# Chunked loads ahead of the last pass, context scaling on GpSimd, PSUM copies on VectorE, and one ring of score banks in a transformer block

## Chip, cores and metric

The kernel runs on one core of one Trainium2 chip, as one launch. The metric is the device time of one execution in microseconds. The profile comes from one profiled execution of the same program on the same kind of core.

## What is computed

One layer of a transformer on an input of 4 batches, 512 positions and 512 features, all float32: attention with 32 query heads in 8 groups of 4 (one key/value head each, head size 16) and a gated feed-forward part of width 1376, both with a layer norm ahead and a residual behind.

```python
q, k, v = split(layernorm(x) @ Wq), split(layernorm(x) @ Wk), split(layernorm(x) @ Wv)
q, k = q * cos + rotate_half(q) * sin, k * cos + rotate_half(k) * sin
att = einsum('bhgqd,bhkd->bhgqk', q, k) / sqrt(16)          # causal mask
x = x + (softmax(att) @ v) @ Wo
xt = layernorm(x)
return x + (silu(xt @ W_gate.T) * (xt @ W_up.T)) @ W_down.T
```

## The kernel before

It has two phases. Phase 1 makes the attention of all four batches, and, in its last pass, the output projection, residual, layer norm and transposition of batch 0. Phase 2 runs the feed-forward part of batch b together with the output projection of batch b + 1. Each float32 operand of the dense products is split in a high part that TensorE reads in one pass (`fp32r`) and the rest, and a product is three matmuls.

**Passes, groups, slots.** `iteration(b, has_next)` is written once for each engine, and the five engines run their own copies. Pass b has 8 groups (one key/value head each, numbered n = 8b + g, so 0 to 31), and a group has 4 slots (`slot = 4g + i`). All order is written by hand: tables name the slot in which a piece of work stands, and an engine works strictly in its own order. In slot i of group n, TensorE (PE) makes the transposed scores of group n for key chunk i (`scores_t`, L1148, into the three-bank ring `ps_t`), the untransposed scores of group n + 2 (`scores`, L1116, into `ps_s`), and in two of the slots the products of the probabilities with V (`weighted_v`, L1161, into `ps_o`). Between them stand pieces of dense work, placed by `gap`: projections of the next batch (L1068, one unit of 12 matmuls per group in groups 0 to 5 or so of a pass), or in pass 3 (batch index B - 1 = 3, groups 24 to 31) the output projection of batch 0 (L1089), from its third group on. Groups 24 and 25 hold no dense pieces.

**The maximum.** VectorE (DVE) reads each bank of `ps_s` for the row maxima of group n + 2 (`row_max`, L872 and L876, 11 banks a group). ACT rounds the 16 maxima of group n + 1 to bf16 (`max_high`), DVE makes the rest (`max_low`, L883, after the first `row_max` of a group), PE transposes both by a matmul with the identity (`transposed_max`, L1132: 32 columns of weights, 128 moving), ACT copies the result (`m_t`, L730), and SP sends it by DMA into rows 96 and 97 of `q_rows` (`stage_max`, L447, slot 1 of a group). Group n + 1 can't begin its `scores_t` until that transfer has landed. ACT takes the exponentials out of `ps_t` (L737), and GpSimd (POOL) masks the diagonal (`mask_probs`, L643 and L645).

**What the change touches.** SP issues all transfers of the loop in one queue, in its written order: `stage_rows` (six DMAs, L434 and L437), `stage_max`, `store_o` (L453), `store_rotated`, and in pass 3 `prepare_batch_0`: at slot 0 the 1 MB of `wo` (L467), two residual tiles (L187) and tile 0 of the attention output with its inverse sums (`load_o`: 8 DMAs of 64 KB, L181 and L182), at slots 4, 8 and 12 the next tiles, at slot 14 the first gate and up weights (L474). DVE scales a tile of that output by the inverse sums (`scale_ctx`, L194, slots 5, 9, 13, 17), ACT makes the high part (L199), DVE the rest (L204). ACT empties `ps_o` (`o_evacuate`, L747) and makes the high part of the transposed x (`xt_high`, L669), DVE its rest (L851).

**Banks.** Banks of `ps_s` are numbered within a group: bank = position % 3, and since a group has 11 positions the first two of a group follow their last users more closely than the rest:

```python
def last_in_bank(k):
    if k >= S_BANKS:
        return k - S_BANKS
    return max(n for n in range(BANKS_OF) if n % S_BANKS == k) - BANKS_OF
```

## Time and profile before

| | |
|---|---|
| median of 3 runs | 793.6 us (790.62 to 796.33) |
| the profiled execution's own time | 795.12 us |
| its span, first to last instruction | 793.4 us |
| granted TensorE clock, mean | 0.978 |
| PE busy | 756.0 us, 95% |
| PE weight loads busy | 510.8 us, 64% |
| DVE busy | 440.7 us, 56% |
| ACT busy | 342.2 us, 43% |
| POOL busy | 211.5 us, 27% |
| phase 1, up to the first matmul of phase 2 | 392.2 us |

The span runs from the first to the last instruction of the profiled execution, and its own time is 1.7 us longer. Busy shares are means over two phases that have different limits, so a stretch must be read by itself. The end of a matmul is modelled: what it really takes, when others follow at once, is the distance from its start to the next start.

### The profile page before, as it was taken

The page shows a single profiled execution, that of the slowest core. Times are in us where ns is not written, and L with a number is a line of the kernel's source. Part 1 is how long each engine was busy: PE and PEld are TensorE (multiplying, and loading weights), DVE is VectorE, ACT ScalarE, POOL GpSimd, SP SyncE. Part 2 cuts the span into 40 slices and gives each one's busy share as a digit, 9 for nine tenths or more (in the row PEclk, how much of TensorE's full clock was granted, in tenths as well). Part 3 has the DMA queues.
Part 4 walks back from the last instruction along what each step waited for, and adds up shares of the span by engine and source line. Part 5 has one row for each costly group of instructions (what it writes and reads, how often), then busy time and mean ns, then how long its engine had stood idle before and what let it go on. Part 6 is the DMA issues. An engine that isn't in the chain of part 4 may idle for free.

```text
span 793.4 us, 12117 instructions
## 1 busy us (share of the span) xinstructions
PE 756.0 (95%) x4209; PEld 510.8 (64%) x4240; DVE 440.7 (56%) x984; ACT 342.2 (43%) x684; POOL 211.5 (27%) x384
## 2 busy tenths in 40 slices
PE   5889999999999997999799999999999999999998
PEld 4634544544444543444488888888888888788886
DVE  6897888688877786898345553233323243241112
ACT  3427767766876776667643322111121111121111
POOL 4236764477446763244300000000000000000000
PEclk9859999999999999799999999999999999999999
DMA  7337676234323435361276200512004120020001
GB/s 264 107 93 241 212 247 209 75 88 121 117 78 100 118 90 189 113 210 42 83 221 205 74 27 4 170 40 80 27 1 162 50 79 26 0 107 0 1 1 53
DMA packets 74613, 81.84 MB, mean 103 GB/s; under 512 B 8720, under 2 KB 58384, under 8 KB 74352
## 3 DMA queue, kind: packets, MB, share of 16 engines
q1 hardware_dynamic: 73264, 79.98, 31.9%
q10 hardware_dynamic: 1296, 1.18, 0.5%
q8 instruction: 30, 0.49, 0.3%
q14 instruction: 23, 0.19, 0.1%
HBM read 57.02 MB, written 33.36 MB: 114 GB/s over the span
## 4 chain that ended last, share of the span: by engine, by line
PE 50%; DVE 0%; issue 0%; DVEq 0%
PE bank L1504 34%; PE ps_y L1556 15%; PE bank L1543 1%; DVE x_in L1486 0%; DVEq L1485 0%
## 5 line engine op out<-in xcount | busy, mean ns | idle before, releaser
L737 ACT ACTIVATE probs<-ps_t 128x512 f32<-128x512 f32 (+1 forms) x352 | 184.2, 562 | 88.5 <-PE ps_t L1148 88.1
L872 DVE CUSTOM_DVE_ANT_0 ps_s<-ps_s,mask_row 128x512 f32<-128x512 f32 (+1 forms) x240 | 145.4, 643 | 43.8 <-PE ps_s L1116 42.7
L1116 PE MATMUL ps_s<-k_rows,q_rows 96*128 96x256 bf16 (+3 forms) x512 | 146.9, 316 | 3.2 <-DVE m_raw L876 1.5
L1461 DVE TENSOR_TENSOR h<-h,bank 128x512 f32<-128x512 f32 (+1 forms) x44 | 30.3, 688 | 214.1 <-PE bank L1504 212.8
L1148 PE MATMUL ps_t<-q_rows,k_rows 98*128 98x512 bf16 (+1 forms) x352 | 129.1, 371 | 8.6 <-DMA q_rows<-m_t 5.8
L1399 ACT ACTIVATE h<-bank 128x512 f32<-128x512 f32 (+1 forms) x44 | 26.3, 597 | 146.3 <-PE bank L1504 146.3
L1161 PE MATMUL ps_o<-probs,v_ones 128*32 128x512 f32 (+3 forms) x1024 | 82.6, 441 | 4.6 <-ACT o_sb L747 0.2
L645 POOL TENSOR_SCALAR_AFFINE_SELECT probs<-probs 128x512 f32<-128x512 f32 x128 | 84.0, 657 | 0.0
L876 DVE TENSOR_REDUCE m_raw<-ps_s 128x2 f32<-128x512 f32 (+3 forms) x112 | 73.3, 678 | 17.4 <-PE ps_s L1121 15.2
L1405 ACT CAST h_hi<-h 128x512 fp32r<-128x512 f32 (+1 forms) x44 | 27.3, 620 | 126.6 <-DVE h L1461 126.6
L226 POOL TENSOR_TENSOR var_eps<-mean_var,eps 128x1 f32<-128x1 f32 x16 | 3.0, 189 | 285.6 <-DVE mean_var L221 285.6
L1116 PEld LDWEIGHTS ps_s<-k_rows,q_rows 96*128 96x128 bf16 x512 | 49.8, 101 | 40.9 <-issue 10.8
L1148 PEld LDWEIGHTS ps_t<-q_rows,k_rows 98*128 98x128 bf16 x352 | 34.6, 99 | 63.6 <-issue 29.3
L643 POOL TENSOR_TENSOR carrier<-half 128x1 f32<-128x1 f32 x128 | 29.0, 227 | 152.3 <-ACT probs L737 151.9
L1556 PE MATMUL ps_y<-wd_hi,h_hi 128*128 128x512 f32 (+1 forms) x176 | 68.8, 391 | 0.0
L1556 PE MATMUL ps_y<-wd_lo,h_hi 128*128 128x512 f32 (+1 forms) x176 | 68.5, 389 | 0.0
L1556 PE MATMUL ps_y<-wd_hi,h_lo 128*128 128x512 f32 (+1 forms) x176 | 68.5, 389 | 0.0
L1161 PEld LDWEIGHTS ps_o<-probs,v_ones 128*32 128x32 f32 x1024 | 27.0, 110 | 43.3 <-issue 31.9
L1504 PE MATMUL bank<-xt_hi,wg_hi 128*128 128x512 f32 (+1 forms) x128 | 50.0, 390 | 0.0
L1504 PE MATMUL bank<-xt_hi,wg_lo 128*128 128x512 f32 (+1 forms) x128 | 49.9, 390 | 0.0
L1504 PE MATMUL bank<-xt_hi,wu_lo 128*128 128x512 f32 (+1 forms) x128 | 49.9, 390 | 0.0
L1504 PE MATMUL bank<-xt_lo,wu_hi 128*128 128x512 f32 (+1 forms) x128 | 49.9, 390 | 0.0
(154 smaller groups left out, 1374.8 us busy)
## 6 DMA issues: line engine op xcount, KB each, us to landing
scratch_o<-o_sb SPq DMA_DIRECT2D x31, 256.0 KB, 2.2
q_rows<-scratch_q_parts SPq DMA_DIRECT2D x32, 192.0 KB
x_in<-in_x SPq DMA_DIRECT2D x16, 256.0 KB, 4.6
q_rows<-scratch_q_parts SPq DMA_DIRECT2D x32, 128.0 KB
x_res<-in_x SPq DMA_DIRECT2D x16, 256.0 KB, 2.7
o_in<-scratch_o SPq DMA_DIRECT2D x64, 64.0 KB
inverse<-scratch_inverse SPq DMA_DIRECT2D x64, 64.0 KB
out<-x_in SPq DMA_DIRECT2D x16, 256.0 KB, 2.0
```

Of the source, the lines that this page charges most:

```text
L643: nc.gpsimd.tensor_tensor(carrier[:, g % 2, c:c + 1], half[:, 0:1], half[:, 0:1], ALU.add)
L645: nc.gpsimd.affine_select(out=diagonal, in_=diagonal, compare_op=ALU.is_ge, fill=0.0, base=0, pattern=[[0, GROUP], [1, P]], channel_multip ...
L737: nc.scalar.activation(probs[:, g % 2, heads * u:heads * (u + 1), CHUNK_AT[c]:CHUNK_AT[c + 1]], ps_t[:, pos % S_BANKS, 0:heads * CHUNK_N[c ...
L872: nc.vector.tensor_tensor_reduce(out=bank, in0=bank, in1=mask_row[:, T - width:T], scale=1.0, scalar=LOWEST, op0=ALU.add, op1=ALU.max, acc ...
L876: nc.vector.tensor_reduce(out=m_raw[:, g % 2, at:at + heads], op=ALU.max, axis=AXIS.X, in_=bank.rearrange("p (j t) -> p j t", j=heads)).th ...
L1116: mm = nc.tensor.matmul(bank[:, place], q_rows[r][0:ROWS, j, P * q:P * (q + 1)], k_rows[r][0:ROWS, 0:width], start=(place == 0), stop=mask ...
L1148: nc.tensor.matmul(ps_t[:, pos % S_BANKS, 0:heads * width], k_rows[r][:, P * c:P * (c + 1)], q_rows[r][:, heads * u:heads * (u + 1), P * c:T],
L1161: mm = nc.tensor.matmul(ps_o[32 * j:32 * j + 2 * DH, P * c:T], v_ones[:, c, g % NKV, :], probs[:, g % 2, j, CHUNK_AT[c]:CHUNK_AT[c + 1]], ...
L1405: nc.scalar.copy(h_parts[0][0:m, r], h[0:m, r]).then_inc(h_hi_ready, 1)
L1461: nc.vector.tensor_tensor(h[0:m, r], h[0:m, r], bank[units["up", f] % BANKS][0:m, :], ALU.mult).then_inc(h_ready, 1)
L1504: mm = nc.tensor.matmul(out, weights(w, c), moving(m, c), start=(c == 0 and n == 0), stop=(c == chunks - 1 and n == 2))
L1556: mm = nc.tensor.matmul(ps_y[:, t], h_parts[w][0:m, r, P * t:P * (t + 1)], wd[p][0:m, f, :], start=(f == 0 and k == 0), stop=(f == FT - 1 ...
```

## The change

- **Loads.** In the pass before the last (`b == B - 2`, batch index 2) SP now issues `wo` in four parts at slots 14, 15, 22 and 23, tiles 0 and 1 of the attention output chunk by chunk (two DMAs a chunk) at slots 2, 3, 6, 7, 10, 11, 18 and 19, and two residual tiles at slots 27 and 31. In pass 3, tiles 2 and 3 come chunk by chunk at slots 9 to 11 and 13 to 15, and the first gate and up weights in four parts at slots 2, 3, 6 and 7.
- **Engines.** `scale_ctx` of phase 1 runs on GpSimd instead of DVE, in the same slots. In pass 3 DVE makes both parts of the transposed x, and copies `ps_o` for groups 29, 30 and 31.
- **Banks.** Banks of `ps_s` form one ring over all groups: bank = (11n + position) % 3.
- **Maximum.** `m_parts` gets six further parts of zeros, so that `transposed_max` has 128 columns of weights; it stands behind the dense piece of its place, not ahead of it; `max_low` stands behind the second `row_max`.
- **Slots.** Layer norm statistics, means and applications, one `rotated` step and the inversion of the sums stand in other slots.

```diff
+LAST_O = {26: 5, 30: 6}
+X_SLOT, MEAN_SLOT = 26, 14
+STATS_AT, APPLY_AT = {6: 0, 7: 1, 10: 2, 11: 3}, {18: 0, 19: 1, 22: 2, 23: 3}
+SUMS_SLOT, INVERSE_SLOT = 7, 18
+WO_LOAD, RESIDUAL_LOAD = (14, 15, 22, 23), (27, 31)
...
-FFN_LOAD, FFN_HI, FFN_LO = 14, 19, 25
+FFN_LOAD, FFN_HI, FFN_LO = (2, 3, 6, 7), 19, 25
...
+def s_place(n, i, u):
+    return BANKS_OF * n + BANK_AT[i] + u
...
-        m_parts = sb("m_parts", [P, 2, 2, GROUP, TT], BF16)
+        m_parts = sb("m_parts", [P, 2, P // (GROUP * TT), GROUP, TT], BF16)
...
+            def prepare_first_tiles(slot):
+                if slot in WO_LOAD:
+                    c = WO_LOAD.index(slot)
+                    if c == 0:
+                        sp.wait_ge(raw_copied, 13 * DMA)
+                    sp.dma_start(to.wo[1][:, c].bitcast(F32), d["wo_raw"][P * c:P * (c + 1)]).then_inc(wo_loaded, DMA)
+                if slot in RESIDUAL_LOAD:
+                    load_residual(sp, d, to, 0, RESIDUAL_LOAD.index(slot))
+                for t, c in O_LOAD_AHEAD.get(slot, ()):
+                    if (t, c) == (0, 0):
+                        sp.wait_ge(inverse_stored, DMA)
+                    load_o_chunk(sp, d, to, 0, t, c)
...
+                    if not has_next and (slot - CTX_SCALE) % TT == 0 and 0 <= slot - CTX_SCALE < TT * TT:
+                        scale_ctx(pool, to, 0, (slot - CTX_SCALE) // TT)
...
+            def last_xt(kc):
+                unit = LAST_UNIT0 + TT + kc
+                dve.wait_ge(dense_ready, unit + 1)
+                nc.vector.tensor_copy(xt_hi[:, kc], dense_bank(unit)).then_inc(xt_hi_ready, 1)
+                xt_low(B, kc, unit)
+
+            def last_output(g):
+                dve.wait_ge(pv_done, NKV * (B - 1) + g + 1)
+                if g < NKV - 1:
+                    dve.wait_ge(o_stored[g % 2], DMA * (NKV // 2 * (B - 1) + g // 2))
+                nc.vector.tensor_copy(o_tile(B - 1, g), ps_o[:]).then_inc(o_evacuated, 1)
...
-                        others.insert(0, lambda: max_low(n + 1))
+                        others[0:0] = [lambda: None, lambda: max_low(n + 1)]
...
-                before = BANKS_OF * n + last_in_bank(BANK_AT[i] + u) + 1
+                before = s_place(n, i, u) - S_BANKS + 1
...
-                nc.tensor.matmul(to[0:2 * GROUP * TT, 0:P], m_parts[:, n % 2].rearrange("p w j q -> p (w j q)"),
+                nc.tensor.matmul(to[:, 0:P], m_parts[:, n % 2].rearrange("p w j q -> p (w j q)"),
```

TensorE's order in group 17, before, from the last scores of slot 0 to the first matmuls of slot 1 (`w_hi` and `w_lo` mark the dense piece, `m_parts` the transposition of the maxima):

```order
L1116 MATMUL ps_s<-k_rows,q_rows 128x512
L1132 MATMUL ps_t<-ident_b,m_parts 32x128
L1068 MATMUL ps_d<-xt_hi,w_hi 128x512
L1068 MATMUL ps_d<-xt_lo,w_hi 128x512
L1068 MATMUL ps_d<-xt_hi,w_lo 128x512
L1148 MATMUL ps_t<-q_rows,k_rows 128x384
```

And the same place in the changed kernel:

```order
L1151 MATMUL ps_s<-k_rows,q_rows 128x512
L1103 MATMUL ps_d<-xt_hi,w_hi 128x512
L1103 MATMUL ps_d<-xt_lo,w_hi 128x512
L1103 MATMUL ps_d<-xt_hi,w_lo 128x512
L1167 MATMUL ps_t<-ident_b,m_parts 128x128
L1183 MATMUL ps_t<-q_rows,k_rows 128x384
```

The transposition has moved behind the dense piece, and writes 128 partitions instead of 32.

The SP queue before, from the end of the row loads in slot 0 of pass 3 (group 24) to the maxima of slot 1 (`q_rows<-m_t`); between the shown pairs on `o_in` and `inverse` stand three more of the same:

```order
L437 DMA q_rows<-scratch_q_parts 16x4x512
L467 DMA wo_lo<-scratch_wo_raw 128x4x512
L187 DMA x_res<-in_x 128x512 x2
L181 DMA o_in<-scratch_o 128x1x128
L182 DMA inverse<-scratch_inverse 128x1x128
```

```order
L181 DMA o_in<-scratch_o 128x1x128
L182 DMA inverse<-scratch_inverse 128x1x128
L447 DMA q_rows<-m_t 2x16x128
L453 DMA scratch_o<-o_sb 128x512
L434 DMA k_rows<-scratch_k_parts 48x1x512
```

The same place in the changed kernel, on to the row loads of slot 4:

```order
L449 DMA q_rows<-scratch_q_parts 16x4x512
L459 DMA q_rows<-m_t 2x16x128
L465 DMA scratch_o<-o_sb 128x512
L496 DMA w_lo<-scratch_wg_raw 128x384
L496 DMA w_lo<-scratch_wu_raw 128x384
L496 DMA w_lo<-scratch_wg_raw 128x384
L496 DMA w_lo<-scratch_wu_raw 128x384
L446 DMA k_rows<-scratch_k_parts 48x1x512
```

The eleven issues between the row loads and the maxima are gone from there, and four parts of the feed-forward weights stand behind the store of the output.

## Rows read from the trace of the kernel before

**Rows 1.** The chain that ended last, by line (page, part 4), and its first long piece.
```profile
PE bank L1504 34%; PE ps_y L1556 15%; PE bank L1543 1%; DVE x_in L1486 0%; DVEq L1485 0%
...
392.21 11.14 PE bank L1504 x48
```

**Rows 2.** Timeline of PE (start us, us, instruction, [idle before <-releaser]): groups 23 to 26 begin.
```profile
296.67 0.39 PE L1148 MATMUL ps_t<-q_rows,k_rows 98*128 98x512 bf16 x1
...
304.79 0.39 PE L1148 MATMUL ps_t<-q_rows,k_rows 98*128 98x512 bf16 x1
...
318.80 0.61 PE L1148 MATMUL ps_t<-q_rows,k_rows 98*128 98x512 bf16 x1 [5.81 <-DMA q_rows<-m_t]
...
330.27 0.39 PE L1148 MATMUL ps_t<-q_rows,k_rows 98*128 98x512 bf16 x1
```

**Rows 3.** Stretches: the two halves of group 25, group 26, group 16.
```profile
core 0: us, PE busy (x) PEld busy (x) DVE busy (x) ACT busy (x) POOL busy (x), PEclk, DMA share, GB/s
...
318.80:326.80 8.00, 8.00 (x34) 2.94 (x35) 6.23 (x18) 4.76 (x11) 0.78 (x2) 0.50 0.39 114
326.80:330.27 3.47, 3.32 (x31) 1.51 (x29) 3.44 (x8) 3.23 (x7) 1.71 (x5) 0.99 0.25 88
330.27:341.15 10.88, 10.73 (x78) 5.27 (x76) 9.90 (x26) 6.84 (x15) 4.48 (x10) 1.00 0.49 144
...
223.21:233.90 10.69, 10.54 (x79) 5.36 (x76) 7.19 (x20) 8.32 (x18) 1.87 (x6) 1.00 0.27 83
```

**Rows 4.** Timeline of the SP queue: last issue of group 23, then group 24.
```profile
300.09 0.67 SPq L447 DMA_DIRECT2D q_rows<-m_t  x1
...
306.06 0.43 SPq L467 DMA_DIRECT2D wo_lo<-scratch_wo_raw  x1
...
314.61 1.15 SPq L447 DMA_DIRECT2D q_rows<-m_t  x1
```

**Rows 5.** DMA issues by line: size of one, median us from issue to landing.
```profile
w_lo<-scratch_wg_raw SPq DMA_DIRECT2D x1, 768.0 KB, 4.7
```

**Rows 6.** Timeline of PE around a transposition of maxima, and later in that group 16.
```profile
225.47 0.38 PE L1116 MATMUL ps_s<-k_rows,q_rows 96*128 96x512 bf16 x1
225.78 0.23 PE L1132 MATMUL ps_t<-ident_b,m_parts 128*32 128x128 bf16 x1
225.94 0.50 PE L1068 MATMUL ps_d<-xt_hi,w_hi 128*128 128x512 f32 x1
226.28 0.39 PE L1068 MATMUL ps_d<-xt_lo,w_hi 128*128 128x512 f32 x1
...
231.50 0.33 PE L1116 MATMUL ps_s<-k_rows,q_rows 96*128 96x128 bf16 x3
231.67 0.38 PE L1148 MATMUL ps_t<-q_rows,k_rows 98*128 98x512 bf16 x1
```

**Rows 7.** Weight loads by line: duration min/median/max, first and last start.
```profile
L1132 PEld LDWEIGHTS ps_t<-ident_b,m_parts x31: 92/93/102, 58.5 to 375.0; 128*32 128x32 bf16 x31
...
L1121 PEld LDWEIGHTS ps_s<-mask_q,ident_b x112: 97/98/152, 40.1 to 371.2; 128*128 128x128 bf16 x112
```

**Rows 8.** GpSimd and VectorE operations by line, columns as in the group above.
```profile
L568 POOL TENSOR_TENSOR rot<-rot,turned x17: 1263/1278/1288, 39.7 to 286.5; 128x512 f32<-128x512 f32 x17
...
L194 DVE TENSOR_TENSOR o_in<-o_in,inverse x16: 674/684/689, 325.0 to 650.6; 128x512 f32<-128x512 f32 x16
...
L883 DVE TENSOR_TENSOR m_parts<-m_raw,m_parts x32: 169/254/1201, 49.0 to 374.5; 128x16 bf16<-128x16 f32 x32
```

**Rows 9.** Timeline of PE and of ACT in group 31.
```profile
383.12 0.34 PE L1148 MATMUL ps_t<-q_rows,k_rows 98*128 98x384 bf16 x1 [1.08 <-ACT probs L737]
...
387.26 0.63 PE L1057 MATMUL ps_d<-ident,xn 128*128 128x128 f32 x4 [1.22 <-DVE xt_lo L851]
...
388.04 2.36 PE L1161 MATMUL ps_o<-probs,v_ones 128*32 128x512 f32 x32
...
381.98 0.59 ACT L669 CAST xt_hi<-ps_d 128x512 fp32r<-128x512 f32 x1
```

More of the change, by code:

```diff
@@ L109, in positive @@
     return not isinstance(count, int) or count > 0
-def last_in_bank(k):
-    if k >= S_BANKS:
-        return k - S_BANKS
-    return max(n for n in range(BANKS_OF) if n % S_BANKS == k) - BANKS_OF
+def s_place(n, i, u):
+    return BANKS_OF * n + BANK_AT[i] + u
 def t_count(n, pos):
@@ new lines, in prepare_batch_0 @@
+            def prepare_batch_0(slot):
+                if slot in FFN_LOAD:
+                    c = FFN_LOAD.index(slot)
+                    if c == 0:
+                        sp.wait_ge(dense_ready, LAST_UNIT0)
+                    for at, name in ((0, "wg_raw"), (FIRST * P, "wu_raw")):
+                        sp.dma_start(w_lo[:, c, at:at + FIRST * P].bitcast(F32),
+                                     d[name][P * c:P * (c + 1), 0:FIRST * P]).then_inc(ffn_loaded, DMA)
+                for t, c in O_LOAD.get(slot, ()):
+                    sp.wait_ge(to.ctx_lo_ready, t - 1)
+                    load_o_chunk(sp, d, to, 0, t, c)
@@ L510, in iteration @@
                         store_inverse(b - 1)
+                    if b == B - 2:
+                        prepare_first_tiles(slot)
                     if not has_next:
@@ L755, in dense_read @@
                 unit = UNIT0[b] + place
-                if kind == "T":
+                if kind == "T" and b < B - 1:
                     xt_high(unit, k)
@@ L771, in iteration @@
                         max_evacuate(n + 1)
-                    if i == PV_EVACUATE and n >= 1:
+                    if i == PV_EVACUATE and n >= 1 and (has_next or slot not in LAST_O):
                         o_evacuate(b, g - 1)
@@ L788, in iteration @@
                         c = slot - WO_HI
-                        act.wait_ge(wo_loaded, DMA)
+                        act.wait_ge(wo_loaded, KC * DMA)
                         nc.scalar.copy(to.wo[0][:, c], to.wo[1][:, c].bitcast(F32)).then_inc(wo_hi_ready, 1)
@@ L792, in iteration @@
                         c = slot - FFN_HI
-                        act.wait_ge(ffn_loaded, 2 * DMA)
+                        act.wait_ge(ffn_loaded, 2 * KC * DMA)
                         nc.scalar.copy(w_hi[:, c], w_lo[:, c].bitcast(F32)).then_inc(ffn_hi_ready, 1)
-                if not has_next:
-                    act.wait_ge(to.ctx_lo_ready, TT)
-                    o_evacuate(b, NKV - 1)
             act.wait_ge(w_loaded["wk"], DMA)
@@ L937, in batch_0_work @@
                     work.append(lambda: split_wo(slot - WO_LO))
-                for at, step in ((CTX_SCALE, lambda t: scale_ctx(dve, to, 0, t)),
-                                 (CTX_LO, lambda t: ctx_low(dve, to, 0, t, first_ctx(t)))):
-                    if (slot - at) % TT == 0 and 0 <= slot - at < TT * TT:
-                        work.append(lambda step=step, t=(slot - at) // TT: step(t))
+                if (slot - CTX_LO) % TT == 0 and 0 <= slot - CTX_LO < TT * TT:
+                    work.append(lambda t=(slot - CTX_LO) // TT: ctx_low(dve, to, 0, t, first_ctx(t)))
+                if slot in LAST_O:
+                    work.append(lambda: last_output(LAST_O[slot]))
                 if slot in LAST_XT:
-                    work.append(lambda: xt_low(B, LAST_XT[slot], LAST_UNIT0 + TT + LAST_XT[slot]))
+                    work.append(lambda: last_xt(LAST_XT[slot]))
                 for after, step in ((0, first_residual), (STATS_AFTER, first_statistics), (MEAN_AFTER, first_mean),
@@ L1179, in iteration @@
                                 weighted_v(b, g + after, c)
+                        for place, kind, k, piece in pieces.get((slot, j), ()):
+                            dense(b + 2 if has_next and kind == "T" else b + 1, kind, k, UNIT0[b] + place, piece)
                         if (i, j) == (0, GROUP - 1) and n + 1 < GROUPS:
                             transposed_max(n + 1)
-                        for place, kind, k, piece in pieces.get((slot, j), ()):
-                            dense(b + 2 if has_next and kind == "T" else b + 1, kind, k, UNIT0[b] + place, piece)
                 if not has_next:
```

61 lines of the change are left out of this document (25 added, 36 removed).

## Prediction

> **What bounds the kernel now.** I read the chain that ended last first. It is a chain of TensorE matmuls from 392.21 us to the end [rows 1]. Phase 2 starts there, and neither its order nor its transfers change, so I leave its 401 us as they are: all of the change must show in the 392.2 us ahead of it.
>
> In phase 1 I then read the timeline of PE, group by group, and the stretches. A full group such as 16 takes 10.69 us, with PE busy for 10.54, DVE for 7.19 and ACT for 8.32 [rows 3]: PE sets the pace, and the others have room. That holds in three passes. The exception is the start of pass 3. Group 24 begins at 304.79 and group 25 only at 318.80, with 5.81 us of idle PE ahead of it, ended by the DMA of the transposed maxima [rows 2]. Without that wait group 24 would have taken 14.01 - 5.81 = 8.2 us. Group 25 then takes 11.47 us, though it holds no dense work either. The stretches say why: for the first 8.0 us the granted clock is 0.50, the 1.2 GHz level, and only in the last 3.5 us is it 0.99 [rows 3]. PE had just been idle for 5.81 us. The groups behind it are PE's again: 10.88 us with 10.73 busy, but now with DVE at 9.90 [rows 3], the second engine to watch.
>
> Why was the DMA late? The SP timeline shows it. In group 23, which began at 296.67, the maxima were issued at 300.09, 3.4 us in. In group 24 SP issues `wo` at 306.06, two residual tiles and eight pieces of the attention output, and reaches the maxima at 314.61: 8.55 us for 11 issues, 0.78 us each. From there to the end of PE's wait at 318.80 are another 4.2 us [rows 2, 4]. The queue of issues, not the amount of data, is what is late.
>
> **The change, part by part.** The sum is made against the profiled execution (span 793.4, own time 795.1); the median of the three runs is 793.6, so I subtract from the median.
>
> *Loads out of slot 0 of pass 3.* SP then reaches the maxima at about 308.1, 3.3 us into the group as in group 23, and even with 4.2 us to land [rows 2, 4] they are there at 312.3, ahead of the 313.0 at which PE wants them. Gain: 5.8 us. It could leave 0.5 us if other transfers slow it.
>
> *Group 25 at full clock.* Without idle time before it PE has no cause to fall. It then needs 8.2 us, as group 24, but DVE was busy for 6.23 + 3.44 = 9.67 us in it [rows 3], since the four steps that split `wo` stand there. Scaling the tile on GpSimd takes one operation of 0.68 us away [rows 8]. So DVE becomes the bound at 9.0 us; I take 9.2. Gain: 11.47 - 9.2 = 2.3 us; between 0.7 (two operations of DVE held up by GpSimd, see below) and 3.3 (PE's 8.2).
>
> *The transposition of the maxima.* This is a small thing that comes in every group. Around it PE's starts are 225.47, 225.78, 225.94, 226.28: 0.31 + 0.16 + 0.34 = 0.81 us [rows 6]. A 512-column matmul is otherwise followed after 0.213 us (512 columns at 2.4 GHz), a 128-column one after 0.17 / 3 = 0.057 us (three stand between 231.50 and 231.67 [rows 6]), and one of the dense products takes 11.14 / 48 = 0.232 us [rows 1]. That is 0.50 us, so 0.31 us are lost around one 32-column matmul. The changed one has 128 columns like its neighbours, and stands ahead of a bf16 matmul whose weights load like those of the 57 ns row. I take 0.27 to 0.31 us less per group, where a float32 piece of the dense work stands in slot 0: 6 groups in each of three passes and 4 in pass 3, 22 in all: 6.4 us. Groups without such a piece wait for an exponential there anyway; I give them nothing. The bounds: 0 if the loss belongs to any such small matmul, 7.5 with all groups.
>
> The Trainium skill (TensorEngine Tiling (Array Packing), Key Properties) says that changing the tiling mode drains TensorE; by that rule the loss is the two changes of mode, and the change removes both. A second rule speaks against it: TensorE: Matmul & The Clock Gate, LDWEIGHTS, has the load time grow with the columns of weights, P / 1.2 ns, which would be 27 ns for 32 columns and 107 for 128, 80 ns more in each of 32 groups, so 2.6 us lost instead of gained.
>
> The trace has both kinds of load: 93 ns median with 32 columns, 98 ns with 128 [rows 7], a difference of 5 ns, or 0.2 us over 32 groups. I take the rows.
>
> Cost of the move: the transposition stands 0.7 us later (one dense piece), `max_low` one `row_max` later. The maxima so reach SP perhaps 0.5 us later. In group 23 they were issued 3.4 us in; with 4.2 to land they have 10.69 - 7.6 = 3.1 us to spare in a full group. Hidden.
>
> *One ring of banks.* The first two banks of a group may be filled one bank earlier. PE shows no waits on them in full groups; 0.2 us, bounds 0 and 1.
>
> *Scaling on GpSimd.* The rope operations show a product of this shape: 1278 ns there [rows 8]. Four of them lie in the middle of groups 25 to 28, where POOL is busy for 4.48 us of 10.88 [rows 3]. ACT reads the result in the next slot, so the 0.6 us more than the 0.68 on DVE are hidden. What is not plainly hidden is that the two engines hold each other up: `max_low`, 169 ns at its shortest, took up to 1201 [rows 8], and GpSimd's rope work is what lies beside it in three passes. Four hold-ups of up to 1.28 us meet a DVE that has 10.5 - 9.3 = 1.2 us free in a group. I charge 0.4 us, bounds 0 and 4.
>
> *Issues added to SP in pass 2.* At most four per group, in full 4 x 0.78 = 3.1 us, against the 3.1 us to spare above; and `store_o` waits for ACT's copy before it, so part of the issues fall in time in which SP had waited. Hidden, but not by much. In pass 3 the four parts of gate and up weights per group are 0.75 MB: 4.7 us to land as one [rows 5], behind the maxima of group 24 and ahead of those that are issued 6 us later. Hidden.
>
> *PSUM copies on DVE in groups 29 to 31.* With no scores to make, PE waits in group 31: 1.08 us for an exponential and 1.22 us for the rest of the transposed x [rows 9]. ACT is the bound, and its copy of 0.5 us at 381.98 stands before the exponential that PE wants. Taking it away brings the first wait down by 0.5 us. The second shrinks since DVE follows the transposition at once, with two operations of some 0.68 us [rows 8]: 0.4 us; group 30 gives 0.3. Behind them PE's last 2.36 us [rows 9], the last copy and its DMA are the same length on either engine. Gain 1.2 us, bounds 0 and 2.5.
>
> Sum: 5.8 + 2.3 + 6.4 + 0.2 - 0.4 + 1.2 = 15.5 us. 793.6 - 15.5 = 778 us.
>
> **The rivals.**
>
> *The small matmul gives nothing.* The 0.31 us could be the price of any matmul with 128 moving columns between long ones, or be replaced by a wait for ACT. For: no row shows one such matmul alone with 128 columns of weights. Against: three in a row do 57 ns each. 778 + 6.4 = 784.5 us.
>
> *A new wait at the start of pass 3 or on the SP queue of pass 2.* The row loads, the weights and the maxima share one queue. If one transposition is late again by 2 to 3 us and the clock falls behind it, a half of the 8.1 us of today comes back; with hold-ups by GpSimd of 2 us, 784 us.
>
> The Trainium skill (SBUF — State Buffer, Terms) says that VectorE and GpSimd share a port pair that one locks and the other waits for; the 1201 ns of `max_low` beside its 169 agree [rows 8].
>
> *The other side: the queue is late in pass 2 again and again.* From the 3.1 us to spare it decides: if the issues of tile chunks cost more than that beside the six row loads and the stores of the rotated rows, the maxima of that group land late. Each such group could cost what group 24 does now: up to 5.8 us and 2.3 us at the low clock behind it. Two eat up the gain; with three of the eight groups the kernel takes 778 + 24 = 802 us. For it: the slack is as large as the cost. Against: the waits of `store_o` give SP time that I haven't counted, and no slot of pass 2 gets more than two issues.
>
> *More than I count.* If DVE does not bound group 25 (1.0 us), all groups gain on the transposition (1.1) and the tail gives 2.5 (1.3 more): 774.7 us.
>
> **How the numbers follow.** The forecast has 0.60 (774 to 782), nothing from the small matmul 0.16, one new wait 0.11, the queue late again and again 0.04, more than counted 0.09. The range from 772 to 787 holds all but the fourth and the edges of the others. About 1% is what a measurement of this kernel can tell from no change: the line is at 785.7. Below it lie the forecast, the last case, and most of the second and third: 0.87. Within 1%: the rest of those, 0.09. Slower: 0.04.
>
> **What would show it.** Phase 2's first matmul at 376 to 378 us. No wait for the maxima's DMA ahead of group 25, and clock 1.00 through pass 3. Full groups at 10.4 us. Group 25 at 9 to 9.5 us with DVE never idle. In group 31 no wait of over 0.7 us for an exponential. I am wrong if full groups stay at 10.69, if PE waits for `m_t` anywhere in passes 2 and 3, or if the masks on POOL come late and PE waits for `probs`.

## The result, and the profile after

The changed kernel takes 778.8 us (median of 4 runs, 777.27 to 780.59) against 793.5 us (median of 4, 790.62 to 796.33) for the kernel before: a ratio of 0.983, with a 95% interval from 0.981 to 0.986. The forecast was 778.0 us. The profiled execution of the changed kernel has an own time of 777.3 us and a span of 775.6. Two slow executions of experiment kernels, at 1078 and 1906 us, are left out of the medians below.

First the page of the changed kernel: busy time by engine, and the chain that ended last.

```profile
span 775.6 us, 12157 instructions
PE 747.3 (96%) x4240; PEld 509.3 (66%) x4240; DVE 443.9 (57%) x988; ACT 338.5 (44%) x677; POOL 217.3 (28%) x388
...
PE 51%; DVE 0%; issue 0%; DVEq 0%
```

Its chain of waits in order of time begins where phase 2 begins:

```profile
374.38 11.16 PE bank L1539 x48
```

Phase 2 begins 17.8 us earlier than in [rows 1] and lasts 401.2 us in both. So all of the difference lies in phase 1, as it had to. Here it is by stretch, in the two profiled executions. A group's length is the time from its first transposed score to that of the next group, or to phase 2.

| stretch | before, us | after, us | gained |
|---|---|---|---|
| up to group 1 | 65.75 | 63.10 | 2.65 |
| groups 1 to 23 | 239.04 | 233.11 | 5.93 |
| group 24 | 14.01 | 8.13 | 5.88 |
| group 25 | 11.47 | 9.81 | 1.66 |
| group 26 | 10.88 | 10.84 | 0.04 |
| groups 27 to 29 | 32.08 | 31.13 | 0.95 |
| groups 30 and 31 | 18.98 | 18.26 | 0.72 |

From group 1 to phase 2 that is 15.2 us. The 17.8 of the two spans holds 2.65 us from the start, and how many of these belong to the change stays open: see the experiments on the ring.

The stretches of the changed kernel, one full group (16) first, then groups 24 to 27 (columns: stretch, length, busy time and count of PE, PEld, DVE, ACT, POOL, granted clock, DMA share, GB/s):

```profile
216.93:227.31 10.38, 10.38 (x79) 5.39 (x76) 7.18 (x20) 8.33 (x18) 1.87 (x6) 1.00 0.23 72
296.21:304.34 8.13, 7.90 (x68) 3.35 (x64) 6.66 (x20) 6.91 (x17) 2.47 (x7) 1.00 0.41 122
304.34:314.15 9.81, 8.16 (x67) 3.40 (x64) 9.17 (x24) 8.07 (x19) 5.99 (x11) 1.00 0.60 186
314.15:324.99 10.84, 10.65 (x80) 5.32 (x76) 9.68 (x25) 6.86 (x15) 4.35 (x10) 1.00 0.45 141
324.99:335.37 10.38, 10.38 (x80) 5.39 (x76) 9.48 (x26) 6.86 (x15) 5.58 (x12) 1.00 0.49 148
```

The full group is 10.38 us with PE busy for all of them, against 10.69 in [rows 3]. The granted clock is 1.00, the 2.4 GHz level, through the start of pass 3, where [rows 3] has 8.0 us at 0.50. Of these, group 25 is the one with much idle PE left: 1.65 us, with DVE busy for 9.17 of 9.81.

### The profile page after: what moved, and what is told of

Same layout as the page of the kernel before. It is cut to its first block, busy times and chain, and to the rows that moved or that the text cites. A ratio compares the mean times of both kernels' runs of the same rounds, so it can differ in the third digit from the quotient of the medians.

```text
span 775.6 us, 12157 instructions
## 1 busy us (share of the span) xinstructions
PE 747.3 (96%) x4240; PEld 509.3 (66%) x4240; DVE 443.9 (57%) x988; ACT 338.5 (44%) x677; POOL 217.3 (28%) x388
## 4 chain that ended last, share of the span: by engine, by line
PE 51%; DVE 0%; issue 0%; DVEq 0%
PE bank L1539 35%; PE ps_y L1591 15%; PE bank L1578 1%; DVE x_in L1521 0%; DVEq L1520 0%
## 5 line engine op out<-in xcount | busy, mean ns | idle before, releaser
L1151 PE MATMUL ps_s<-k_rows,q_rows 96*128 96x256 bf16 (+3 forms) x512 | 143.4, 308 | 4.5 <-DVE m_raw L892 2.0
L1183 PE MATMUL ps_t<-q_rows,k_rows 98*128 98x512 bf16 (+1 forms) x352 | 126.7, 364 | 1.7 <-ACT probs L760 1.6
L896 DVE TENSOR_REDUCE m_raw<-ps_s 128x2 f32<-128x512 f32 (+3 forms) x112 | 72.9, 674 | 15.5 <-PE ps_s L1156 15.1
L1196 PEld LDWEIGHTS ps_o<-probs,v_ones 128*32 128x32 f32 x1024 | 26.9, 109 | 42.5 <-issue 33.1
```

What stands on the lines that cost most here:

```text
L896: nc.vector.tensor_reduce(out=m_raw[:, g % 2, at:at + heads], op=ALU.max, axis=AXIS.X, in_=bank.rearrange("p (j t) -> p j t", j=heads)).th ...
L1151: mm = nc.tensor.matmul(bank[:, place], q_rows[r][0:ROWS, j, P * q:P * (q + 1)], k_rows[r][0:ROWS, 0:width], start=(place == 0), stop=mask ...
L1183: nc.tensor.matmul(ps_t[:, pos % S_BANKS, 0:heads * width], k_rows[r][:, P * c:P * (c + 1)], q_rows[r][:, heads * u:heads * (u + 1), P * c:T],
L1196: mm = nc.tensor.matmul(ps_o[32 * j:32 * j + 2 * DH, P * c:T], v_ones[:, c, g % NKV, :], probs[:, g % 2, j, CHUNK_AT[c]:CHUNK_AT[c + 1]], ...
```

## The experiments

Each is an edit of one of the two kernels; `before` and `after` in a heading say of which. The ratio is always to the kernel before, run beside it on the same chip.

### The transposition: its width alone, and its place alone

Width (before, with the weights of the transposition 128 columns wide):

```diff
-        m_parts = sb("m_parts", [P, 2, 2, GROUP, TT], BF16)
+        m_parts = sb("m_parts", [P, 2, P // (GROUP * TT), GROUP, TT], BF16)
+            nc.vector.memset(m_parts[:, :, 2:], 0.0)
-                nc.tensor.matmul(to[0:2 * GROUP * TT, 0:P], m_parts
+                nc.tensor.matmul(to[:, 0:P], m_parts
```

> The kernel before with one edit: the transposition of the maxima has 128 columns of weights instead of 32 (zeros behind the maxima), in its old place ahead of the dense piece. Theory (the 0.31 us lost around it come from the narrow matmul between wide ones): the distances 0.31 and 0.16 us around it fall to about 0.22 and 0.06, full groups from 10.69 to about 10.5 us, the run 4 us shorter. Rival (any short matmul ahead of a float32 weight load costs this, and only the place matters): full groups stay at 10.69 us, time within 1 us of before.

Place (before, with the transposition still 32 columns wide but behind the dense piece):

```diff
-                        if (i, j) == (0, GROUP - 1) and n + 1 < GROUPS:
-                            transposed_max(n + 1)
                         for place, kind, k, piece in pieces.get((slot, j), ()):
                             dense(...)
+                        if (i, j) == (0, GROUP - 1) and n + 1 < GROUPS:
+                            transposed_max(n + 1)
```

> The kernel before with one edit: the transposition of the maxima, still 32 columns wide, stands behind the dense piece. Theory of the narrow matmul: the losses on entering and leaving it stay (0.09 and 0.10 us), and only the 0.10 us of the dense piece's first matmul is won: full groups 10.6 us, the run 2 us shorter. Rival (only the place matters): full groups 10.38 us as in the changed kernel, the run 7 us shorter.

Measured: width 786.2 us, ratio 0.993 (0.990 to 0.996), most full groups at 10.43 us. Place 788.3 us, ratio 0.997 (0.994 to 1.000, so it can't be told from no change by the times), most full groups at 10.57 us. Against 10.69 that is 0.26 and 0.12 us a group; both together, in the changed kernel, 0.31. The width's median fell by 5.9 us, more than the 4.4 us that its 20 full groups show in its profile. Groups 24 to 26 are also 2.8 us shorter there than in the profile before, which need not be the width's doing: the stall in them differs from one profile to the next (see the loads alone).

The timelines of PE from the last scores of slot 0 to slot 1 show how (start us, us, instruction). Width alone:

```profile
221.37 0.38 PE L1117 MATMUL ps_s<-k_rows,q_rows 96*128 96x512 bf16 x1
221.59 0.22 PE L1133 MATMUL ps_t<-ident_b,m_parts 128*128 128x128 bf16 x1
221.62 0.48 PE L1069 MATMUL ps_d<-xt_hi,w_hi 128*128 128x512 f32 x1
221.93 0.40 PE L1069 MATMUL ps_d<-xt_lo,w_hi 128*128 128x512 f32 x1
```

Place alone:

```profile
224.02 0.39 PE L1068 MATMUL ps_d<-xt_hi,w_lo 128*128 128x512 f32 x1
224.34 0.23 PE L1132 MATMUL ps_t<-ident_b,m_parts 128*32 128x128 bf16 x1
224.50 0.34 PE L1148 MATMUL ps_t<-q_rows,k_rows 98*128 98x384 bf16 x1
```

The changed kernel:

```profile
219.19 0.38 PE L1151 MATMUL ps_s<-k_rows,q_rows 96*128 96x512 bf16 x1
219.22 0.58 PE L1103 MATMUL ps_d<-xt_hi,w_hi 128*128 128x512 f32 x1
219.63 0.39 PE L1103 MATMUL ps_d<-xt_lo,w_hi 128*128 128x512 f32 x1
219.86 0.39 PE L1103 MATMUL ps_d<-xt_hi,w_lo 128*128 128x512 f32 x1
220.09 0.23 PE L1167 MATMUL ps_t<-ident_b,m_parts 128*128 128x128 bf16 x1
220.16 0.33 PE L1183 MATMUL ps_t<-q_rows,k_rows 98*128 98x384 bf16 x1
```

In [rows 6] the transposition starts 0.31 us after the scores ahead of it and holds what follows for 0.16. With 128 columns it starts 0.22 us (width alone) or 0.23 us (changed kernel) after the matmul ahead of it, and holds what follows for 0.03 or 0.07. With 32 columns in the new place it still starts 0.32 us after the float32 matmul ahead of it, where 0.23 is the usual distance, and holds what follows for 0.16. So about 0.09 us are lost on the way into 32 columns and 0.09 to 0.13 on the way out, wherever it stands. The Trainium skill (TensorEngine Tiling (Array Packing), Key Properties) says that a change of tiling mode drains TensorE; these rows agree in that time is lost at both changes, some 0.2 us for the pair, though a drain as such is not to be seen in them. The place alone is worth 0.12 us with the narrow one and 0.05 beside the wide one. The rival that the small matmul gives nothing is out: 18 of the 20 full groups (1 to 5, 8 to 13, 16 to 21, 27 to 29) win 0.31 us or a little more, and all 20 together 5.8 us.

Groups 4 and 12 win only 0.03 and 0.07 us. In group 4 of the changed kernel `max_low`, a step of 0.17 us when nothing lies beside it, stands next to a product of GpSimd's rope work:

```profile
96.12 1.28 POOL L589 TENSOR_TENSOR rot<-raw,cos 128x512 f32<-128x512 f32 x1
96.15 1.29 DVE L903 TENSOR_TENSOR m_parts<-m_raw,m_parts 128x16 bf16<-128x16 f32 x1
```

It takes 1.29 us, and the transposition behind it starts 3.26 us into the group instead of 3.16. In group 12 it is 1.32 us, and 3.29. Before, it was held up for at most 1.20 us, in group 21 [rows 8], and no transposition started later for it.

### The eight issues ahead of the maxima

Before, with the eight transfers of tile 0 of the attention output moved from slot 0 to slot 1, behind the maxima; `wo` and the two residual tiles stay ahead of them:

```diff
-                t = (slot - O_LOAD) // TT
-                if slot == O_LOAD + TT * t and t < TT:
+                at = O_LOAD + 1 if slot < TT else O_LOAD
+                t = (slot - at) // TT
+                if slot == at + TT * t and 0 <= t < TT:
```

> The kernel before with one edit: the eight transfers of tile 0 of the attention output leave slot 0 of pass 3 and stand in slot 1, behind the maxima; wo (1 MB) and two residual tiles (0.5 MB) stay in slot 0 ahead of the maxima. Theory (SP's issues are what is late): the maxima are issued at about 308.2 us of the span instead of 314.6, TensorE waits under 1 us ahead of group 25, the clock stays up, and 7 to 8 us are won. Rival (the bytes ahead in the queue are what is late): 1.5 of 2 MB are still ahead, the maxima land 5 us or more after their issue, and TensorE waits 2 us or more with the lower clock behind it; 0 to 3 us are won.

Measured: 789.8 us, ratio 0.998 (0.996 to 1.000). Its stretches, groups 24 to 26:

```profile
304.50:312.62 8.12, 7.82 (x66) 3.35 (x64) 6.66 (x20) 6.72 (x16) 2.45 (x7) 1.00 0.85 271
312.62:324.90 12.28, 8.53 (x66) 3.30 (x63) 10.33 (x26) 8.25 (x19) 4.31 (x10) 1.00 0.49 149
324.90:335.58 10.68, 10.53 (x74) 5.40 (x75) 9.05 (x24) 6.84 (x15) 3.06 (x8) 1.00 0.45 136
```

Its SP queue (start us, us, engine, line, transfer): the maxima of group 24, the eight issues now behind them, and those of group 25.

```profile
307.29 0.65 SPq L447 DMA_DIRECT2D q_rows<-m_t  x1
307.99 0.67 SPq L181 DMA_DIRECT2D o_in<-scratch_o  x1
308.70 0.61 SPq L182 DMA_DIRECT2D inverse<-scratch_inverse  x1
...
322.90 0.70 SPq L447 DMA_DIRECT2D q_rows<-m_t  x1
```

And PE at the end of group 25:

```profile
324.90 0.39 PE L1149 MATMUL ps_t<-q_rows,k_rows 98*128 98x512 bf16 x1 [2.34 <-DMA q_rows<-m_t]
```

Group 24 falls from 14.01 to 8.12 us with the 1.5 MB still ahead of the maxima: the issues were late, not the bytes. But the lateness moved on. The eight issues, the row loads and the next eight stand one after the other, the maxima of group 25 leave at 322.90, 10.3 us into the group, and PE waits 2.34 us for them. Without a wait group 25 takes 9.65 us (the next experiment), so the same queue took back 2.6 of the 5.9 us one group later. Groups 24 to 26 take 31.1 us here, 36.4 in the profiled execution before, and 28.9 in the next experiment. Two numbers that I lacked come out of it: with little ahead of them the maxima land within 2.0 us of their issue (322.90 to 324.90, where I had 4.2), and after 2.34 us of idle PE the clock stayed at 1.00.

### The loads alone

Before, with all the loads of the changed kernel (those in pass 2, tiles 2 and 3 by chunks, the weights in four parts) and nothing else of it. The core of the edit:

```diff
-                    if not has_next:
-                        prepare_batch_0(slot)
+                    if b == B - 2:
+                        prepare_first_tiles(slot)
+                    if not has_next:
+                        prepare_batch_0(slot)
```

> The kernel before with one part of the change: the loads (wo, residuals and tiles 0 and 1 from pass 2, the others chunk by chunk in pass 3, the feed-forward weights in four parts). Scaling stays on VectorE. Theory: group 24 takes 8.12 us, no wait for the maxima, clock 1.00; group 25 is bound by VectorE, at 10.1 us as in the changed kernel with the scaling on VectorE; groups 26 to 29 at 10.7 to 10.9; together 7.3 us won, 785 us. Rival (the added issues make the maxima late somewhere in pass 2 or in groups 25 to 28): TensorE waits for them over 1 us in one of these groups, and under 6 us are won.

Measured: 787.5 us, ratio 0.995 (0.993 to 0.997). Groups 24 to 26:

```profile
305.33:313.45 8.12, 7.97 (x68) 3.35 (x64) 6.66 (x20) 6.91 (x17) 2.46 (x7) 1.00 0.43 129
313.45:323.10 9.65, 8.47 (x67) 3.27 (x64) 9.01 (x25) 8.01 (x19) 4.28 (x10) 1.00 0.58 181
323.10:334.23 11.13, 10.94 (x79) 5.26 (x76) 10.14 (x26) 6.84 (x15) 3.11 (x9) 1.00 0.47 143
```

The stall is gone and nothing came in its place. From group 1 to phase 2 this kernel takes 319.0 us, 7.5 less than the profiled execution before; by the medians it is 4.2 us. The loads are worth 4 to 7.5 us, and one reason for the spread is seen in the other profiles. In the profiled execution before, group 24 took 14.01 us and group 25 11.47. In the three other kernels that still have the stall (width, place and ring alone) group 24 took 12.54, 13.92 and 13.77, and group 25 10.10, 10.69 and 10.24. What one stall costs behind it thus varies from 0.5 to 1.8 us against the 9.65 of this kernel, and the execution that I had as evidence was the costliest of four. The granted clock says the same: it was low for some 3.5, 6.5 and 3.5 us behind the stall in these three and for 8.0 in the profile before. Here is the ring alone, from the start of group 25:

```profile
315.04:318.04 3.00, 3.00 (x8) 1.08 (x8) 1.86 (x6) 1.89 (x4) 0.00 (x0) 0.50 0.46 143
```

### The ring, and the start of the kernel

The ring alone (before):

```diff
+def s_place(n, i, u):
+    return BANKS_OF * n + BANK_AT[i] + u
-                bank = ps_s[:, (BANK_AT[i] + u) % S_BANKS, 0:heads * width]
+                bank = ps_s[:, s_place(n, i, u) % S_BANKS, 0:heads * width]
-                before = BANKS_OF * n + last_in_bank(BANK_AT[i] + u) + 1
+                before = s_place(n, i, u) - S_BANKS + 1
```

> The kernel before with one edit: the banks of the untransposed scores form one ring over all groups. Theory: in the start, where VectorE's reductions set the pace, TensorE doesn't wait at the change of group 0 to 1, its clock is at the upper level some us earlier, and group 1 begins at about 63.5 instead of 65.75 us; nothing changes in full groups (10.69 us). The run is about 2 us shorter. Rival (the start won its 2.65 us by the wider transposition or by chance of the transfers): group 1 begins at 65.5 to 66 us, time as before.

The changed kernel without it (the same lines back):

> The changed kernel with the old banks of the untransposed scores (numbered anew in each group). Theory: group 0 goes from 9.64 back to 11.0 to 11.2 us since TensorE waits for VectorE's reductions at the change from group 0 to 1 and its clock rises later; full groups stay at 10.38 us; 1.3 us lost. Rival (with shorter full groups the ring is needed in all of them): full groups at 10.45 us or more, 3 us or more lost.

The changed kernel once more, unchanged:

> The changed kernel again, beside the two others on the same chip, to compare with the version that goes further and to see how far its start differs from one execution to another. Group 1 began 22.95 us after the first scores in its first profile. Theory (the ring takes away the wait at the change from group 0 to 1, and the clock rises sooner): again 22.9 to 24.1 us. Rival (the early rise of the clock was chance): 25 us or more, as in four of the five kernels with the old banks.

Measured: the ring alone 791.7 us, ratio 1.000 (0.998 to 1.003), full groups unchanged at 10.69. Without the ring 781.8 us, ratio 0.989 (0.985 to 0.993), full groups of 10.38, group 0 of 10.54 (with it 9.64 in the first profile and 11.20 in the second) and group 31 of 11.45 (11.21 in both). The changed kernel again 777.95 us, ratio 0.983 (0.981 to 0.985).

What the start is worth is seen from the two profiles of the same program. Their stretches just ahead of group 0, first the changed kernel, then the same kernel again:

```profile
49.00:53.00 4.00, 3.10 (x17) 1.06 (x15) 4.00 (x9) 0.26 (x1) 0.00 (x0) 0.86 0.26 71
53.00:57.00 4.00, 4.00 (x23) 2.19 (x23) 4.00 (x11) 2.43 (x6) 0.27 (x2) 1.00 0.49 152
```

```profile
49.00:53.00 4.00, 3.41 (x14) 1.07 (x13) 4.00 (x9) 0.64 (x3) 0.00 (x0) 0.50 0.11 31
53.00:57.00 4.00, 4.00 (x18) 2.21 (x16) 3.68 (x7) 0.87 (x3) 0.00 (x0) 0.50 0.73 217
```

In the first the clock rises to the 2.4 GHz level within 49 to 53 us, in the second only after 57. Group 1 begins at 63.10 in the one and at 66.50 in the other, and their own times differ by as much: 777.27 and 780.74. From group 1 to phase 2 they take 311.3 and 311.4 us. So the 2.65 us of the table's first line are for the most part the moment at which the clock rose in one execution, and the second execution of the same program does not have them. Of the ring itself one wait can be seen to go, 0.50 us at 47.63 in the kernel before, for a maximum of DVE. Whether the ring makes an early rise more likely stays open. Of seven profiled executions with the ring, the first scores stand 23.0 to 24.0 us ahead of group 1 in four and 25.3 to 26.7 in three; of six without it, 25.5 to 26.9 in all (of the five that the last expectation speaks of, all, and not four). The medians do not agree with each other either: the ring alone gives nothing, its loss in the changed kernel costs 3 to 4 us.

Part of that loss lies where no bank of `ps_s` is in use. The profile without the ring has an own time 3.8 us longer than the changed kernel's first: 1.8 us up to group 1, 0.5 from there to phase 2, and 1.5 in phase 2, which takes 402.7 us there and 401.1 to 401.2 in the twelve other profiles. Its first matmul of phase 2, and a stretch behind it:

```profile
376.66 0.47 PE L1546 MATMUL bank<-xt_hi,w_hi 128*128 128x512 f32 x1 [2.12 <-PEq L265]
...
378.66:380.66 2.00, 2.00 (x6) 1.52 (x6) 0.65 (x1) 0.62 (x1) 0.00 (x0) 0.50 0.75 215
```

PE is idle for 2.12 us at the change of phase, where it is 1.81 to 1.88 in the others, and the granted clock then falls to 0.50. The longer pause is also the whole difference in group 31. Whether it comes with the old banks or by chance can't be told from one profile.

### GpSimd's scaling, and an earlier split of `wo`

Both on the changed kernel. Scaling back on DVE:

```diff
-                    if not has_next and (slot - CTX_SCALE) % TT == 0 and 0 <= slot - CTX_SCALE < TT * TT:
-                        scale_ctx(pool, to, 0, (slot - CTX_SCALE) // TT)
+                for at, step in ((CTX_SCALE, lambda t: scale_ctx(dve, to, 0, t)),
+                                 (CTX_LO, lambda t: ctx_low(dve, to, 0, t, first_ctx(t)))):
```

> The changed kernel with the scaling of the attention output back on VectorE, all else as changed. Theory (in the changed kernel GpSimd's product at 308.23 holds up VectorE's split of wo, 1.37 instead of 0.69 us, and TensorE waits 1.43 us behind it): without it the split takes 0.69 us again, but VectorE has an operation of 0.68 us more in group 25, so group 25 stays at 9.6 to 10.0 us (9.81 in the changed kernel), and the run is within 1 us of the changed kernel. Rival (moving the product off VectorE is worth its 0.68 us in each of groups 25 to 28): group 25 at 10.4 us or more and the groups behind it longer than 10.38 us, 2 us or more lost.

Split of `wo` earlier, ACT's copies from slot 0 on instead of 2 and DVE's differences from slot 1 on instead of 4:

```diff
-WO_HI, WO_LO, CTX_SCALE, CTX_HI, CTX_LO = 2, 4, 5, 6, 7
+WO_HI, WO_LO, CTX_SCALE, CTX_HI, CTX_LO = 0, 1, 5, 6, 7
```

> The changed kernel with the split of wo three slots earlier: ScalarE's copies in slots 0 to 3 of pass 3 instead of 2 to 5, VectorE's differences in slots 1 to 4 instead of 4 to 7. Theory (group 25 is bound by VectorE): group 24 goes from 8.13 to 8.3 to 8.8 us, group 25 from 9.81 to 8.2 to 8.6, group 26 from 10.84 to 10.4, so phase 2 begins 1.2 to 1.8 us earlier. Rival (TensorE's wait in group 25 comes from GpSimd's product wherever the splits stand): group 25 stays over 9.3 us and under 0.7 us is won.

Measured: scaling on DVE 778.15 us, ratio 0.984 (0.981 to 0.987), group 25 of 10.13. Split early 778.2 us, ratio 0.982 (0.979 to 0.986). The changed kernel, group 25, from its timelines of POOL, DVE and PE:

```profile
308.23 1.27 POOL L206 TENSOR_TENSOR o_in<-o_in,inverse 128x512 f32<-128x512 f32 x1
...
308.68 1.37 DVE L914 TENSOR_TENSOR wo_lo<-wo_lo,wo_hi 128x512 fp32r<-128x512 f32 x1
...
310.64 0.28 PE L1151 MATMUL ps_s<-k_rows,q_rows 96*128 96x256 bf16 x1 [1.43 <-DVE m_raw L892]
```

The same step of DVE with the scaling on DVE:

```profile
307.89 0.69 DVE L912 TENSOR_TENSOR wo_lo<-wo_lo,wo_hi 128x512 fp32r<-128x512 f32 x1
```

While POOL has its product DVE's step takes twice its time, the maximum behind it comes late by as much, and PE waits 1.43 us. The Trainium skill (SBUF — State Buffer, Terms) says that the two engines share a port pair that one locks; 1.37 beside 0.69 us for the same step agree. For all that the scaling on GpSimd still wins 0.3 us net in group 25: on DVE the scaling itself takes 1.16 us there, and PE waits 0.74 and 0.83 us for maxima. Neither reaches the 9.65 us of the loads alone, which also scale on DVE. So something else in the change costs group 25 about 0.5 us; which part was not tested.

With the split early, no step on `wo` lies beside POOL's product. Groups 24 to 26 of that kernel:

```profile
300.50:309.06 8.56, 8.05 (x67) 3.34 (x64) 7.92 (x23) 7.80 (x19) 2.45 (x7) 1.00 0.38 114
309.06:317.63 8.57, 8.16 (x67) 3.35 (x64) 8.23 (x23) 7.02 (x17) 5.62 (x11) 1.00 0.65 201
317.63:328.00 10.37, 10.37 (x79) 5.40 (x76) 8.59 (x23) 6.85 (x15) 4.73 (x10) 1.00 0.50 155
```

27.5 us instead of 28.8: group 25's excess comes from DVE's work on `wo` in it. How much of the 1.3 us is GpSimd's hold-up and how much the work itself, the edit does not separate, since it moves both away. The median does not show the 1.3 us, as four runs that spread over 4 us can't; its profiled execution had the late rise of the clock (26.6 us from the first scores to group 1). Nor does the profile show it in sum: from group 1 to phase 2 it takes 311.4 us, as the changed kernel does, for it lost 1.2 us in group 4 (11.85 us for 10.66), in pass 0, which the edit doesn't touch. PE at its end:

```profile
109.12 0.39 PE L1183 MATMUL ps_t<-q_rows,k_rows 98*128 98x512 bf16 x1 [1.39 <-DMA q_rows<-m_t]
```

That is a wait for the maxima, see the part on the SP queue below.

### The tail's copies back on ACT

The changed kernel with ACT's copies in groups 29 to 31 as before:

```diff
-                    if kind == "T" and b < B - 1:
+                    if kind == "T":
-                if i == PV_EVACUATE and n >= 1 and (has_next or slot not in LAST_O):
+                if i == PV_EVACUATE and n >= 1:
```

> The changed kernel with the last groups' PSUM copies back on ScalarE (both the high parts of the transposed x and the outputs of groups 29 to 31). Theory (ScalarE's copies ahead of the exponentials are what TensorE waits for): groups 30 and 31 go from 7.05 and 11.21 us back to 7.3 and 11.7, 0.7 us later, not to be seen in the times. Rival (the copies weigh more now that the groups before are shorter): 1.5 us or more lost.

Measured: 778.6 us, ratio 0.984 (0.981 to 0.988). Groups 30 and 31 take 7.29 and 11.69 us again, as before the change, instead of 7.05 and 11.21: the copies on DVE are worth 0.72 us. PE's waits in group 31 of the changed kernel:

```profile
365.28 0.34 PE L1183 MATMUL ps_t<-q_rows,k_rows 98*128 98x384 bf16 x1 [0.59 <-ACT probs L760]
...
369.37 0.41 PE L1092 MATMUL ps_d<-ident,xn 128*128 128x128 f32 x2 [1.17 <-DVE xt_lo L871]
```

And what DVE does ahead of the second:

```profile
367.81 0.69 DVE L941 CAST xt_hi<-ps_d 128x512 fp32r<-128x512 f32 x1 [0.95 <-PE ps_d L1092]
368.53 0.69 DVE L871 TENSOR_TENSOR xt_lo<-ps_d,xt_hi 128x512 fp32r<-128x512 f32 x1
```

The first wait of [rows 9] is halved, from 1.08 to 0.59 us. The second stays: 1.17 instead of 1.22. The two parts still follow one another, 0.69 + 0.69 us on DVE; before, ACT's part took 0.59 us and DVE's 0.69 behind it.

### The early split, with wider gaps between the transpositions of x

On the changed kernel, the early split of `wo`, and the four transpositions of x set wider apart:

```diff
-NEXT_T = [("T", 0, 32), ("T", 1, 34), ("T", 2, 36), ("T", 3, 38)]
-NEXT_XT = {26: 0, 27: 1, 29: 2, 31: 3}
+NEXT_T = [("T", 0, 32), ("T", 1, 35), ("T", 2, 37), ("T", 3, 39)]
+NEXT_XT = {26: 0, 28: 1, 30: 2, 31: 3}
```

> The changed kernel with the split of wo three slots earlier and the transpositions of x in passes 0 and 1 at gaps 32, 35, 37 and 39 instead of 32, 34, 36 and 38 (VectorE's halves in slots 26, 28, 30, 31). Theory: groups 24 to 26 win 1.3 us as in the run with the early split alone; groups 6 and 14, where TensorE waited 0.95 us for VectorE's half of the first transposed x, win that wait, so groups 6 and 7 together go from 19.6 to 18.7 us, the same in pass 1. Phase 2 begins 3 us earlier than in the changed kernel with an equal start: about 775.5 us. Rival (the two last transpositions, now two slots apart at the end of group 7, wait instead): groups 6 and 7 together stay at 19.6 us, and only 1.3 us are won.

Measured: 778.7 us, ratio 0.985 (0.982 to 0.987): no better. Groups 24 to 26 keep the gain (8.57, 8.56, 10.39), but groups 6 and 7 take 20.85 us instead of 19.62, and 14 and 15 take 20.13. PE's wait for the rest of the transposed x is still there, 0.92 us at 136.18 (0.95 in the changed kernel, the wait that the wider gaps were to remove), and it now also waits for ACT's copy (0.43 us at 126.09) and for the maxima (0.66 us at 128.46). Which of the moved steps delays these two was not traced further.

## Why the prediction was right, and where not

**Group 24: right, 5.9 us for 5.8.** No PE wait on the maxima in passes 2 and 3, in any profile of the changed kernel or its variants, and the issues were the cause. My 4.2 us to land was too long, and with little in flight it is 2.0; this made the step safer than I thought.

**Group 25: the term was mis-sized on both ends.** I had 11.47 - 9.2 = 2.3 us, and it is 1.66 in the two profiles, some 0.3 to 0.9 against the group's 10.1 to 10.7 us in the other kernels with the stall. The end of 9.2 us missed 0.6: I had DVE's busy time as the length, but PE waits 1.43 us for a maximum that GpSimd's product has made late by about 0.7. I had charged hold-ups in a term of their own (below). The other end was a single execution whose low clock cost more than the others' did. I took its 8.0 us at the low clock as a property of the kernel.

**Transposition: right.** 0.31 us in a full group, the top of my 0.27 to 0.31, and nothing where no dense piece stands in slot 0 (groups 24, 7 and 15). In sum it is 5.8 us and not 6.4: 20 groups for my 22, since group 26 gains nothing and group 0 is part of the start, and groups 4 and 12 lose their share to a held-up `max_low`, where I had taken the cost of its move as hidden. Mechanism and split were tested: most of it is the width. The weight load of the changed kernel's transposition, by line (duration in ns, min/median/max):

```profile
L1167 PEld LDWEIGHTS ps_t<-ident_b,m_parts x31: 95/96/96, 56.7 to 357.9; 128*128 128x128 bf16 x31
```

With 32 columns it took 93 ns [rows 7]. The rule of the Trainium skill that I weighed (TensorE: Matmul & The Clock Gate, LDWEIGHTS: load time grows with the columns) does not hold here: 3 ns, not 80.

**What I gave nothing, and what gave less.** Groups 6 and 14 fell from 10.93 to 10.62 us and group 22 from 9.31 to 8.89, in all 1.0 us. Width and place alone leave them at 10.92 and 9.32, as do the loads, and without the ring they stay at 10.63 and 8.88. So it comes from the edits left over, the slots of the layer norm steps or of `max_low`, or from width and place only together. That was not tested apart. In group 22 the trace shows what went: a wait of PE for a row maximum in the kernel before,

```profile
293.15 0.28 PE L1116 MATMUL ps_s<-k_rows,q_rows 96*128 96x256 bf16 x1 [0.35 <-DVE m_raw L872]
```

which the changed kernel no longer has. On the other side group 26 won 0.04 us and not 0.3: DVE has 9.68 us of work in it, the end of the split of `wo` included, and the early split, which takes that out, brings it to 10.37.

**Ring: 0.2 us predicted, nothing measured in full groups, open for the start.** With the ring alone groups 1 to 23 take 239.0 us, as before. The 2.65 us at the start I had not predicted, and the second profile of the changed kernel does not have them: its group 1 begins later than before the change.

**Scaling on GpSimd: the hold-ups cost about what I charged, in a place where I had not put them.** The term of -0.4 us was for hold-ups alone; the step saved on DVE stood in group 25's term. One hold-up is seen to reach PE, the 0.7 us of group 25, and it fits the 0.6 us by which that group missed. So the two terms must be read together: 2.3 - 0.4 = 1.9 us for 1.66. That the whole move wins 0.3 us net is another comparison, which my sum did not make.

**Tail: mis-sized, 0.72 us for 1.2.** The first wait behaved (0.49 for 0.5). The step that failed is the second, 0.4 us because "DVE follows the transposition at once": that saved nothing, since ACT's part had been as short.

**The SP queue in pass 2: no loss, but my slack was read in the wrong group.** I read that the maxima leave 3.3 us into a group, and there are groups in which they leave at 7.0 us before the change already, since the stores of the rotated rows stand ahead of them. The changed kernel's queue in group 18, which begins at 237.69:

```profile
237.66 2.51 SPq L399 DMA_DIRECT2D scratch_k_parts<-r_top  x4
240.22 1.17 SPq L399 DMA_DIRECT2D scratch_k_parts<-r_low  x2
...
244.84 0.68 SPq L459 DMA_DIRECT2D q_rows<-m_t  x1
```

The maxima leave 7.15 us in, 3.2 us ahead of group 19, and land in time. In group 20 it is 7.15 against 5.2 before. The rival that this queue is late again and again did not come, but it was nearer than a chance of 0.04 says: some 1.2 us, from the 2.0 that a transfer takes to land, and not 3.1.

The queue did come late in pass 0, which I had not looked at. In group 4 the maxima left 6.2 us into the group before, and leave 7.6 to 8.9 us in with the changed kernel and its variants, 8.5 in its first profile. That profile has no wait for them. The second has waits of 0.23 and 0.09 us, ahead of groups 3 and 5; the early split has 1.39, and there the maxima took 3.0 us from issue to the start of group 5. With the loads, the width or the place alone they leave at 6.3 to 6.4. The likely cause is the `rotated` step that moved by one slot, from 13 to 14: its three stores now stand in the queue close ahead of the next three. That was not tested. My term for the move had the maxima 0.5 us later, which holds in most groups and not in this one.

The sum came out at 15.2 us from group 1 to phase 2 for my 15.5, with errors of up to 1.0 us in single terms, in both directions. That it also met the median within 0.8 us owes something to chance: my sum stood on an execution 1.5 us slower than the median, and I took the 15.5 off the median. The medians fell by 14.7. The median of three that I subtracted from was itself high: in 41 further runs, on three chips, the kernel before has medians of 791.7 to 792.1 us. Beside the changed kernel's second set of runs it is 791.65 us, and the gain 13.7.

## What to carry to other kernels

A small transfer that gates the next group must not stand in a queue behind many issues: count issues, not bytes, and follow them one group further than the one you mend, since moving eight issues by one slot won 5.9 us and lost 2.6 again behind it. And follow them in every pass that an edit touches, in more than one profile: moving one small step by a slot seems to have brought the same lateness to pass 0. A lone narrow matmul among full-width ones cost TensorE about 0.2 us on top of itself here, and padding its weights with zeros to the full width cost nothing that could be seen (a load of 96 ns instead of 93). And when a stall leaves a low clock behind it, take the cost of the clock from several executions, not from the one at hand.

## What the hardware did that I had not expected

- The moment at which the clock first rises to 2.4 GHz differs between executions of the same program (within 49 to 53 us, and after 57), and makes 3.4 us of their own times. The runs of this kernel spread over 3 to 4 us.
- The length of a pause alone did not say whether the clock falls behind it. 2.34 us of idle PE left the granted clock at 1.00 in one kernel, and 2.12 us brought it to 0.50 in another. 5.81 us brought it to 0.50 for 8.0 us. Groups of otherwise equal work behind such a stall took 10.10 to 11.47 us.
- A product on GpSimd over SBUF doubled a step of DVE that began 0.45 us after it (0.69 to 1.37 us), and TensorE waited 1.43 us for the maximum behind that step. A step of 128x16 elements, 0.17 us by itself, took 1.29 us beside one.
